# A graph kernel whose TensorE packs each block one step later and directly ahead of the products in front of it

## The reference

```
A   = adj * (y @ y.T)                       # only neighbours of the same class
A   = A / max(rowsum(A), 1e-12)
x1  = layernorm(x + 0.9 * (A @ x) + 0.1 * h0)
h2  = tanh(x1 @ W_proj + b_proj)
new = the 350 largest entries of each row of tanh(adj*adj) * (adj > 0)   # all of them: rows have fewer
out = layernorm(x1 + relu(new @ (h2 @ W_gcn) + b_gcn))
```

## Time and profile before

| | |
|---|---|
| median of three runs | 457.06 us |
| the profiled execution | 457.84 us, its span 456.0 us |
| TensorE matmul busy | 429.3 us (94%) |
| VectorE busy | 379.3 us (83%) |
| ScalarE busy | 266.4 us (58%) |
| GpSimd busy | 160.4 us (35%) |
| read from HBM | 105.57 MB, nearly all of it in the first 23 of 40 slices |

### The profile page before, as it was taken

How to read it: one execution, slowest core, us unless ns; L and a number is a source line. 1 busy time by engine, 2 the same in 40 slices (tenths; PEclk the granted TensorE clock), 3 DMA queues, 4 the chain that set the end, 5 groups by cost and what they waited for, 6 DMA issues and landing times.

```text
span 456.0 us, 15178 instructions
## 1 busy us (share of the span) xinstructions
PE 429.3 (94%) x5143; PEld 381.8 (84%) x5143; DVE 379.3 (83%) x1363; ACT 266.4 (58%) x363; POOL 160.4 (35%) x310
## 2 busy tenths in 40 slices
PE   3669999999999999999999999999999999999994
PEld 2448998888988888888889888888888888888884
DVE  4988999999999999999999997886657667666663
ACT  4997999998999999999999973840000000000000
POOL 3011543544455544455444544132121121221221
PEclk9986999999999999999999999999999999999999
DMA  8999999999999999999999600000000000000000
GB/s 284 412 415 425 404 413 413 402 403 414 413 419 425 418 424 422 428 414 423 418 416 424 254 2 2 8 17 12 18 17 12 17 17 12 17 16 13 17 14 26
DMA packets 25518, 108.49 MB, mean 238 GB/s; under 512 B 5097, under 2 KB 15490, under 8 KB 15490
## 3 DMA queue, kind: packets, MB, share of 16 engines
q1 hardware_dynamic: 25330, 108.13, 58.7%
q10 hardware_dynamic: 160, 0.01, 0.0%
HBM read 105.57 MB, written 2.56 MB: 237 GB/s over the span
## 4 chain that ended last, share of the span: by engine, by line
PE 80%; DVE 12%; issue 5%; POOL 1%; POOLq 0%; DVEq 0%; ACT 0%
PE acc L574 66%; PE words L508 6%; DVE a_bits L880 4%; DVE turned L970 2%; PE feat_acc L641 2%; PE proj_acc L657 2%; PE xnt_acc L633 1%; PE gram_acc L574 1%; PE acc L691 1%; DVE g_words L345 1%; DVE z_high L1038 1%; POOL rstd L455 0%; DVE same_class L993 0%; DVE stats L1051 0%; DVE mean_var L1056 0%
## 5 line engine op out<-in xcount | busy, mean ns | idle before, releaser
L574 PE MATMUL acc<-x_parts,turned 128*128 128x257 f16 x1560 | 188.6, 277 | 4.5 <-DVE turned L970 3.3
L761 ACT ACTIVATE count_out<-a_rows,ones 128x2688 bf16<-128x2688 f32 (+1 forms) x80 | 190.2, 2377 | 0.5
L574 PEld LDWEIGHTS acc<-x_parts,turned 128*128 128x128 fp8e4 x1560 | 152.1, 99 | 27.0 <-issue 5.1
L574 PE MATMUL acc<-f_parts,turned 128*128 128x256 f16 x1480 | 160.8, 271 | 0.0
L574 PEld LDWEIGHTS acc<-f_parts,turned 128*128 128x128 fp8e4 x1480 | 143.2, 98 | 16.7 <-issue 0.4
L880 DVE TENSOR_SCALAR a_bits<-a_rows 128x2688 bf16<-128x2688 f32 (+1 forms) x80 | 116.5, 1456 | 0.8 <-DMA a_rows<-in_adj_dram 0.5
L452 POOL TENSOR_TENSOR var_eps<-mean_var,consts 128x1 f32<-128x1 f32 x79 | 18.4, 233 | 256.6 <-DVE mean_var L1056 129.6
L970 DVE TENSOR_SCALAR turned<-a_words 128x320 uint16 (+1 forms) x304 | 66.2, 231 | 48.0 <-PE acc L574 47.7
L455 POOL TENSOR_TENSOR rstd<-var_eps,consts 128x1 f32<-128x1 f32 x79 | 87.4, 1106 | 6.2
L970 DVE TENSOR_SCALAR turned<-same_class 128x320 uint16<-128x320 uint16 x313 | 71.4, 253 | 0.1
L508 PEld LDWEIGHTS words<-pack,a_bits 128*128 128x128 bf16 (+1 forms) x1600 | 51.6, 97 | 9.0 <-DVE a_bits L880 7.0
(11 more groups left out here) (138 smaller groups left out, 306.9 us busy)
## 6 DMA issues: line engine op xcount, KB each, us to landing
a_rows<-in_adj_dram SPq DMA_DIRECT2D x39, 1344.0 KB, 7.3
a_rows<-in_adj_dram SPq DMA_DIRECT2D x39, 1156.0 KB, 7.7
out_dram<-xn SPq DMA_DIRECT2D x39, 64.0 KB, 1.5
h_rows<-in_L_gnn_h_dram SPq DMA_DIRECT2D x19, 128.0 KB, 7.5
xs<-in_x_dram SPq DMA_DIRECT2D x3, 640.0 KB, 10.3
xs<-in_x_dram SPq DMA_DIRECT2D x1, 512.0 KB, 8.9
y_nat<-in_L_gnn_y_dram SPq DMA_DIRECT2D x1, 304.0 KB, 3.8
a_rows<-in_adj_dram SPq DMA_DIRECT2D x1, 84.0 KB
```

The lines of the kernel that those rows point to most:

```text
L574: mm = pe.matmul(sums_of(n, par)[0:m, used], bits, parts[:, b, used], start=first and b == blocks[0], stop=last and b == blocks[-1])
L761: act.activation(count_out[0:m, 0:w], a_rows[par][h][0:m, 0:w], ACT.Relu, bias=ones[0:m, 0:1], scale=-HUGE, accum_out=col).then_inc(s_coun ...
```

## The change

From step 13 to step 40 the steps get other contents; the numbers of instructions stay.

- TensorE at step t: packs half 0 of block t-1, transposes, half 0 of the products of block t-2, the two small products, packs half 1 of block t-1, half 1 of the products of block t-2. Packing stands ahead of the products, and of block t-1 in place of block t.
- VectorE at step t (`near_step`): cast of half 0 of block t-1, mask of block t-2, its eight unpacks in one run, then row work of block t-3 with `low_features` and `normalize_block` among it, the cast of half 1 of block t-1, the statistics.
- ScalarE copies the words of block t-2 and counts block t-1.
- Step 12 is the turn: nothing is cast, counted, packed, copied, masked or unpacked in it; the products of block 10 and the row work of block 9 are done.
- At the end VectorE begins the first unpacked block of the second layer (`unpack(NB, ...)`) with four of eight bits at step 40 between `add_high` and `add_low`, and the other four at step 41 (before: all at step 40).

What each engine takes at step t:

```
+    TURN_AT = FIRST - 1
...
+    def close(t):
+
+        return not isinstance(t, int) or t > TURN_AT
+
+    def arriving(t, par, pair):
+
+        if close(t):
+            return t - 1, (par + 1) % 2, pair if par == 1 else pair - 1, valid(t - 1)
+        return t, par, pair, valid(t) and t < TURN_AT
+
+    def to_mask(t):
+
+        if close(t):
+            return t - 2, valid(t - 2)
+        return t - 1, valid(t - 1) and t < TURN_AT
```

TensorE:

```
+                near = close(t) and not (isinstance(t, int) and t > NB)
+                p, p_par, _, packs = arriving(t, par, pair)
...
-                elif started:
+                elif started and not near:
                     products(t - 2, par, 0)
-                if valid(t):
-                    pack_rows(t, par, rows_of(t), 0)
+                if packs:
+                    pack_rows(p, p_par, rows_of(p), 0)
...
+                if near:
+                    products(t - 2, par, 0)
...
-                if started:
+                if started and not near:
                     products(t - 2, par, 1)
...
-                if valid(t):
-                    pack_rows(t, par, rows_of(t), 1)
+                if packs:
+                    pack_rows(p, p_par, rows_of(p), 1)
+                if near:
+                    products(t - 2, par, 1)
```

ScalarE (half 1 is counted in the same way):

```
-                if valid(t - 1) and not (isinstance(t, int) and t <= 1):
-                    words_of(t - 1, odd)
+                c, c_par, c_pair, counts = arriving(t, par, pair)
+                w, copies = to_mask(t)
+                if copies and not (isinstance(t, int) and t <= 1):
+                    words_of(w, par if close(t) else odd)
...
-                if valid(t):
-                    count_zeros(t, par, pair, 0, rows_of(t))
+                if counts:
+                    count_zeros(c, c_par, c_pair, 0, rows_of(c))
```

VectorE (the step as it was stays for the other t, without casts, mask and unpacks at step 12):

```
+            def near_step(t, par, pair):
+                odd = (par + 1) % 2
+                c, c_par, c_pair, _ = arriving(t, par, pair)
+                cast(c, c_par, c_pair, 0)
+                mask(t - 2, par)
+                dve.wait_ge(s_masked, t - 1)
+                unpack(t - 2, par, rows_of(t - 2), same_class[:, :].rearrange("p (b w) -> p b w", w=WORDS), 0, BITS)
+                row_scale(t - 3, odd, P)
+                low_features(t - 7, P)
+                row_inverse(t - 3, P)
+                normalize_block(t - 4, par)
+                add_high(t - 3, odd, P)
+                if isinstance(t, int) and t == NB:
+                    unpack(NB, 0, P, words_at(0), 0, BITS // 2)
+                add_low(t - 3, odd, P)
+                cast(c, c_par, c_pair, 1)
+                row_stats(t - 3, odd, P)
+                row_moments(t - 3, odd, P)
...
+                if close(t) and not (isinstance(t, int) and t > NB):
+                    near_step(t, par, pair)
+                    return
...
-                begin(NB, 0, BITS // 2, BITS)
+                begin(NB + 1, 0, BITS // 2, BITS)
```

More of the change, by code:

```diff
@@ L823, in step @@
                     act.activation(xn_t[:, 0:m5], xnt_acc[:, 0:m5], ACT.Copy).then_inc(s_xnt_sb, 1)
-                if valid(t):
-                    count_zeros(t, par, pair, 1, rows_of(t))
+                if counts:
+                    count_zeros(c, c_par, c_pair, 1, rows_of(c))
                 if isinstance(t, int) and t == 1:
@@ L983, in normalize, with class_words_ready @@
                                          rstd[par][0:m, :], ALU.subtract, ALU.mult)
+            def class_words_ready(q):
+                dve.wait_ge(*gram_copied(q * GRAMS - 1))
+                dve.wait_ge(*gram_copied(q * GRAMS - 2))
             def mask(n, par):
[L987 to L990, removed]
+                if isinstance(n, int) and n in (0, PART):
+                    class_words_ready(n // PART + 1)
                 dve.wait_ge(s_words, n + 1)
@@ L1093, in step @@
                     return
-                if valid(t):
+                if close(t) and not (isinstance(t, int) and t > NB):
+                    near_step(t, par, pair)
+                    return
+                if isinstance(t, int) and t == TURN_AT:
+                    class_words_ready(NB // PART)
+                if valid(t) and t < TURN_AT:
                     cast(t, par, pair, 0)
@@ L1097, in step @@
                     low_features(t - 7, rows_of(t - 7))
+                u, masks = to_mask(t)
+                u_par = par if close(t) else odd
                 def bits(lo, hi):
-                    if valid(t - 1):
-                        unpack(t - 1, odd, rows_of(t - 1), same_class[:, :].rearrange("p (b w) -> p b w", w=WORDS), lo, hi)
+                    if masks:
+                        unpack(u, u_par, rows_of(u), same_class[:, :].rearrange("p (b w) -> p b w", w=WORDS), lo, hi)
                 def begin(t_of, u, lo, hi):
@@ L1108, in begin @@
                         unpack(u + NB, u % 2, rows_of(u), words_at(u), lo, hi)
-                begin(NB, 0, 0, BITS // 2)
-                if valid(t - 1):
-                    mask(t - 1, odd)
+                if masks:
+                    mask(u, u_par)
                 if valid(t - 4):
@@ L1116, in step @@
                     low_features(NB - 3, P)
-                if valid(t - 1):
-                    dve.wait_ge(s_masked, t)
+                if masks:
+                    dve.wait_ge(s_masked, u + 1)
                 bits(0, 2)
```

## The result

The changed kernel takes 478.27 us (median of four runs, 477.87 to 478.88) against 456.97 us for the kernel before on the same chip: a ratio of 1.0452 [1.0432, 1.0473]. The forecast was 465.2 us and its range ended at 471.5. The side was right; the loss is 21.3 us where 8.2 were forecast.

A forecast was written before the change was run, and what follows sets the result against it. VectorE's instruction list was taken as the bound, DMA right below. Its step growing from 6.24 to 6.53 us delays block 38's bits by 7.4 us, with the end 8.2: 465.2 us, range 455.5 to 471.5.

The forecast's parts named there:

- VectorE's list is the bound, and its step decides: First stage: VectorE's instruction order sets the step, 6.24 us before, forecast 6.53; each 0.1 us is 2.8 us of time.
- The pairs, +0.39: VectorE's step: uncovered mask to unpack +0.12, high to low sum +0.12, statistics to moments +0.15 us.
- the wait for the inverse deviation goes, -0.10: VectorE's step: normalisation now stands over 3 us after the moments, so its wait for GpSimd disappears, -0.10 us.
- No instruction is added or removed; the order decides: Premise of VectorE's step sum: only times from one instruction's start to the next change, 6.24 to 6.53 us.
- GpSimd, 0.4 as now: VectorE's step: meetings with GpSimd's copy and two products keep costing 0.4 us; bounds from none to 0.87.
- worse: Rival on VectorE's step: all three GpSimd instructions meet the unpacks, and the mask too; 6.7 to 7.0 us, 470 to 478, chance 0.14.
- Step 12, which the prediction calls the turn: Changeover to the new order: block 12's cast at 96.8 us, its count about 99.8; +0.5 us once, DMA's delay hidden.
- From the last cast to block 38's bits 3.6 us: End of first stage, VectorE: cast 1.5, mask 0.35, unpacks 1.3 and 0.4 for GpSimd, from 273.6 to 277.2 us.
- The end, +0.8: TensorE behind block 38's bits: remaining packing +0.55, transpose -0.1, wait for the cast +0.3 us.
- TensorE waits some 0.5 us a step: In the loop TensorE waits for VectorE some 0.5 us a step, and nobody waits for TensorE.
- DMA's share did fall below 1: Sign forecast for the loop: DMA's share, 1.01 before, falls below 1.
- DMA alone for the next bound below VectorE: First stage: DMA lies right below VectorE's list, reading a step's 2.62 MB at 422 GB/s in 6.2 us.

The follow-up runs named there:

- e1: The kernel before with only VectorE's new instruction order, old lag, TensorE and ScalarE as before: 479.45 us, ratio 1.0484.
- e3: The kernel after with VectorE's steps 13 to 38 written out in place of the loop of two steps: 469.7 us, ratio 1.0271.
- e6: The kernel after, loop kept, with the moments of block t-4 moved behind the next step's first cast: 465.64 us, ratio 1.0175.
- e4: The kernel after with GpSimd's copy, h0 product and residual done on one column of 128: 462.82 us, ratio 1.012.
- e5: The kernel before with GpSimd's copy, h0 product and residual done on one column of 128: 454.68 us, ratio 0.9938.
- e10: The kernel before, loop kept, with VectorE's statistics, moments and low sum moved so every short pair has an instruction between: 457.74 us, ratio 1.0003.

## Why the prediction was right in direction and wrong in size

- *VectorE's list is the bound, and its step decides: right.* By e1 the order of its list alone makes the loss.
- *The pairs, +0.39: right.* After has mask to unpack 0.35 and 0.44, high to low 0.37 and 0.47, statistics to moments 0.44; *the wait for the inverse deviation goes, -0.10: right* (mask to normalisation no longer exists, and the normalisation has no wait).
- *"No instruction is added or removed; the order decides": this step of VectorE's sum failed.* It counted engine instructions only. Before, three unpacks with nothing to wait for stand between the moments and the turn, and the turn shows as no more than 0.11 us in every second step (0.54 against 0.43 from these unpacks to the next cast):

```profile
156.55 0.52 DVE L970 TENSOR_SCALAR turned<-same_class 128x320 uint16<-128x320 uint16 x3
156.98 1.55 DVE L880 TENSOR_SCALAR a_bits<-a_rows 128x2688 bf16<-128x2688 f32 x1
...
162.89 0.51 DVE L970 TENSOR_SCALAR turned<-same_class 128x320 uint16<-128x320 uint16 x3
163.43 1.56 DVE L880 TENSOR_SCALAR a_bits<-a_rows 128x2688 bf16<-128x2688 f32 x1
```

These unpacks went, and the turn came to stand behind a waiting instruction. Priced at nothing, it measures 0.35 us a step (7.01 to 6.66 in e3), 9 us over the loop. That the unpacks had hidden it is argued from these rows and from e6, which hides about half of it again.
- *GpSimd, 0.4 as now: under-sized.* It is 0.56 (e4), +0.14 a step against the 0.42 that was read off two meetings, within the bounds given (up to 0.87). The mechanism was foreseen in the "worse" rival: GpSimd is released in front of the long cast and runs straight into the unpacks. The Trainium skill (SBUF — State Buffer, section Who interferes with whom) says that the loser of the port pair that the two engines share blocks for a whole instruction; the trace agrees in kind, with 1.96 us for an inverse deviation beside a cast. The blocking at its worst, 1.15 us, is not reached: eight unpacks pay half of it.

The step, made up again: 6.24 + 0.39 - 0.10 + 0.35 + 0.14 = 7.02; measured 7.01. It closes better than its terms are known: 6.24 already holds some 0.05 of the loop's 0.35, and what GpSimd costs in before was never measured. From the cast of block 12 to that of block 39 it was 96.31 to 285.16 us, where 96.8 and 273.6 were forecast: the last cast comes 11.6 us late, nearly all of the 12.2 us by which the profiled execution exceeds its forecast.

- *Step 12, which the prediction calls the turn: right.* Block 12's cast at 96.31 (96.8), the count of block 12 at 98.90 (99.8), DMA's gap hidden by 1.1 us at block 14, whose first half was requested at 101.74, landed 7.5 us later at 109.3 and was cast from 110.39 on.
- *From the last cast to block 38's bits 3.6 us: right* (285.16 to 288.73). *The end, +0.8: somewhat low*, 189.4 - 188.1 = +1.3.
- *TensorE waits some 0.5 us a step: low.* The waits of TensorE in after, 110 to 270 us, in place of 14 times for 3.3 us:

```profile
PE acc L591 <- DVE turned L995: 20.1, 23, 1.2
```

0.9 a step; in the loop VectorE doesn't wait for TensorE all the same. DMA's share did fall below 1, to 0.98.

The range failed with the step: its upper end of 471.5 us stands for a step of 6.53 + 6.3 / 28 = 6.76 us, and no term in it allowed for the loop. The rival "worse", 6.7 to 7.0 us and 470 to 478, came within 0.3 us of the time, but by luck: it put all of the excess on GpSimd, which has 0.14 of it, and left out the loop, which has 0.35.

The prediction also took DMA alone for the next bound below VectorE. By e5 and e10 TensorE, busy 99% and waiting for nobody, stands there too.

## What to carry to other kernels

Before moving short independent instructions out of a gap, look at everything that they cover, and look for the loop's turn: an instruction that waits, or one just behind, is the wrong place for it. End a turn with a long instruction ahead that depends on nothing recent, or with several that do not wait. Of an engine whose instructions lengthen those of another, ask not only whether it overlaps but which instructions its whole burst will fall on when its release moves; an edit made for another reason can move it too, as in e6. And before filling holes of one engine, read the next bound from a control, and read all of its waits: here DMA and TensorE stood some 0.07 us a step below VectorE (6.17 against 6.24), so a list shortened to about 6 us gained nothing.

## What was not expected of the hardware

The loop's turn showed a hole of 0.34 us at VectorE in after and 0.11 more in every second step of before, with the same loop. GpSimd's inverse deviation took 1.96 us beside a cast and 0.64 released at a cast's end (e6):

```profile
184.19 0.64 POOL L472 TENSOR_TENSOR rstd<-var_eps,consts 128x1 f32<-128x1 f32 x1
```

And writing out VectorE's loop, which took 8.6 us from after, added 2 us to before.
